# VectorE sums the softmax's exponents and takes their reciprocals behind all four low parts of the probabilities

## The reference, cut to what matters

```
q, k, v = xn @ Wq + bq, ctx @ Wk + bk, ctx @ Wv + bv     # xn is the normalised x; ctx is 8 x 1601 x 384
attn = softmax(q @ k.T / sqrt(32))                       # per batch and head: 64 x 1601
out  = attn @ v
x    = x + out @ Wo + bo
x    = x + moe(layernorm(x))                             # top 2 of 8 experts, 512 -> 2048 -> 512
```

## Time and profile before

| what | us |
|---|---|
| time, median of 3 runs | 1180.52 |
| the profiled execution's own time | 1178.61 |
| its span, first to last instruction | 1176.8 |
| TensorE busy | 1134.3 (96%) |
| VectorE busy | 980.9 (83%) |
| ScalarE busy | 728.4 (62%) |
| GpSimd busy | 499.8 (42%) |
| mean granted TensorE clock | 0.993 |

### The profile page before, as it was taken

How to read it: one execution, slowest core, us unless ns; L and a number is a source line. 1 busy time by engine, 2 the same in 40 slices (tenths; PEclk the granted TensorE clock), 3 DMA queues, 4 the chain that set the end, 5 groups by cost and what they waited for, 6 DMA issues and landing times.

```text
span 1176.8 us, 25102 instructions
## 1 busy us (share of the span) xinstructions
PE 1134.3 (96%) x8110; PEld 1081.3 (92%) x8110; DVE 980.9 (83%) x2286; ACT 728.4 (62%) x1505; POOL 499.8 (42%) x440
## 2 busy tenths in 40 slices
PE   4899999999999999999999999998999999999996
PEld 3799999999999999999999999986999999999996
DVE  6568888888889888888888888877888888888886
ACT  3455656656565656566565656654677777777774
POOL 6356555646546564655565564351112011111111
PEclk9899999999999999999999999999999999999999
DMA  5231212122121212121212211034787887878874
GB/s 185 82 92 42 64 54 60 57 59 60 43 72 40 64 49 64 47 65 46 62 40 72 64 40 44 27 130 144 215 270 234 267 247 235 234 244 270 239 234 117
DMA packets 82062, 137.49 MB, mean 117 GB/s; under 512 B 11513, under 2 KB 36217, under 8 KB 82033
## 3 DMA queue, kind: packets, MB, share of 16 engines
q1 hardware_dynamic: 78496, 129.12, 34.7%
q0 software_dynamic: 3536, 8.00, 3.4%
HBM read 129.96 MB, written 7.14 MB: 117 GB/s over the span
## 4 chain that ended last, share of the span: by engine, by line
PE 89%; DVE 5%; ACT 3%; issue 1%; DMA 1%; DVEq 1%; POOL 0%; ACTq 0%; SPq 0%; POOLq 0%
PE ps L1580 16%; PE ps L417 13%; PE ps L419 12%; PE ps L418 12%; PE ps L1426 8%; PE ps L1483 8%; PE ps L1581 6%; PE ps L1464 5%; PE ps L1465 4%; PE ps L1573 1%; PE ps L1415 1%; ACT y_gated L890 1%; PE ps L1616 1%; DMA wq_raw<-in_wq_dram 1%; DVE k_mix L987 1%
## 5 line engine op out<-in xcount | busy, mean ns | idle before, releaser
L555 POOL TENSOR_TENSOR ctx_hi<-ctx_raw,no_query 128x1152 fp32r<-128x1152 f32 x64 | 142.9, 2233 | 297.1 <-PE ps L419 287.5
L987 DVE SCALAR_TENSOR_TENSOR k_mix<-ps,bk_sb,k_mix 64x384 fp32r<-64x384 f32 (+1 forms) x256 | 162.2, 634 | 84.4 <-ACT k_mix L727 80.5
L767 ACT ACTIVATE probs<-ps,negmax 128x1152 f32<-128x1152 f32 x64 | 78.4, 1225 | 203.9 <-DVE negmax L1085 203.9
L417 PE MATMUL ps<-wv_hi,ctx_hi 128*128 128x256 f32 (+1 forms) x624 | 181.7, 291 | 6.7 <-DVE k_mix L987 6.5
L559 POOL TENSOR_TENSOR ctx_lo<-ctx_raw,ctx_hi 128x1152 fp32r<-128x1152 f32 x64 | 179.8, 2810 | 5.0
L419 PE MATMUL ps<-wv_hi,ctx_lo 128*128 128x256 f32 (+1 forms) x624 | 175.7, 282 | 0.0
L418 PE MATMUL ps<-wv_lo,ctx_hi 128*128 128x256 f32 (+1 forms) x624 | 175.2, 281 | 0.0
L727 ACT ACTIVATE k_mix<-ps,bk_sb 64x384 fp32r<-64x384 f32 (+1 forms) x256 | 150.9, 590 | 22.7 <-PE ps L419 18.0
L1580 PE MATMUL ps<-xg_mix,w_hi 128*128 128x320 f32 x584 | 163.3, 347 | 1.1 <-DVE h_sum L1262 1.1
L1580 PE MATMUL ps<-h_mix,w_hi 128*128 128x320 f32 x576 | 161.3, 349 | 2.7 <-DVE h_mix L1268 1.9
L1098 DVE TENSOR_TENSOR pt_mix<-ps,pt_mix 128x384 fp32r<-128x384 f32 (+1 forms) x256 | 138.7, 583 | 7.0 <-ACT pt_mix L778 5.0
(11 more groups left out here) (217 smaller groups left out, 2714.4 us busy)
## 6 DMA issues: line engine op xcount, KB each, us to landing
w_raw<-in_w_dram SPq DMA_DIRECT2D x76, 1024.0 KB, 6.1
ctx_raw<-in_ctx_t_dram SPq DMA_DIRECT2D x48, 576.0 KB, 3.8
ctx_raw<-in_ctx_t_dram SPq DMA_DIRECT2D x16, 673.5 KB, 4.1
out_dram<-acc POOLq DMA_DIRECT2D x2, 1024.0 KB, 10.6
q_both<-q_scratch SPq DMA_DIRECT2D x14, 128.0 KB, 3.0
x<-in_x_dram SPq DMA_DIRECT2D x1, 1024.0 KB, 5.6
wq_raw<-in_wq_dram SPq DMA_DIRECT2D x1, 1024.0 KB, 8.1
q_scratch<-q_out SPq DMA_DIRECT2D x1, 1024.0 KB, 6.2
```

The costliest lines, as they stand in the source:

```text
L417: pe.matmul(acc_ap, a_hi, b_hi, start=start, stop=False)
L555: nc.gpsimd.tensor_tensor(ctx_hi[slot][:, :, 0:n], ctx_raw[slot][:, :, 0:n], no_query[:].rearrange("p (o i) -> p o i", o=1).broadcast_to([ ...
L987: last = nc.vector.scalar_tensor_tensor(out=k_mix[other, 2 * a + i, cols], in0=ps[rows, bank, 0:m], scalar=bk_sb[rows, a:a + 1], in1=k_mix ...
```

## The change

The sum moves from in front of the four low parts to behind them, with its wait for the exponents, and the two reciprocals with their wait for the sum move from between the first and the second low part to behind the sum. Nothing else is changed, and the number of instructions is the same.

```diff
-                dve.wait_ge(exp_done, 2 * n + 2)
-                nc.vector.tensor_reduce(total[:], rowsum[:], AX.X, ALU.add).then_inc(total_ready, 1)
                 for c in range(CHUNKS):
                     dve.wait_ge(pt_high, CHUNKS * n + c + 1)
                     m = CHUNK_TILES[c]
                     nc.vector.tensor_tensor(pt_mix[:, TILE0[c]:TILE0[c] + m, 1, :],
                                             ps[:, SCORE_BANK + c, 0:m * P].rearrange("p (t r) -> p t r", t=m),
                                             pt_mix[:, TILE0[c]:TILE0[c] + m, 0, :].bitcast(F32),
                                             ALU.subtract).then_inc(pt_split, 1)
-                    if c == 0:
-                        dve.wait_ge(total_ready, n + 1)
-                        for h in range(2):
-                            rows = slice(h * HALF, (h + 1) * HALF)
-                            part = nc.vector.reciprocal(rinv_all[rows, h, s:s + 1], total[rows, :])
-                        part.then_inc(diag_ready, 1)
+                dve.wait_ge(exp_done, 2 * n + 2)
+                nc.vector.tensor_reduce(total[:], rowsum[:], AX.X, ALU.add).then_inc(total_ready, 1)
+                dve.wait_ge(total_ready, n + 1)
+                for h in range(2):
+                    rows = slice(h * HALF, (h + 1) * HALF)
+                    part = nc.vector.reciprocal(rinv_all[rows, h, s:s + 1], total[rows, :])
+                part.then_inc(diag_ready, 1)
                 if s == 0 and before is not None:
                     normalise(before[0])
```

## The result

The changed kernel takes 1183.32 us, median of 12 runs (1181.3 to 1184.0), against 1179.63 us for the kernel before, also 12 (1178.22 to 1181.28). The ratio is 1.0028, with a 95% interval of 1.0020 to 1.0035: 2.4 to 4.1 us slower. In the profiled executions the spans are 1180.0 and 1176.8 us, 3.2 apart. The forecast was 1181.2 us, +0.7, inside a range of -2.7 to +5.7. It had given that outcome, slower by more than 0.2%, 22%, and 68% to no change.

A forecast was written before the change was run, and what follows sets the result against it. VectorE and ScalarE were taken to pace ordinary steps, TensorE only steps 60 to 63. 7.1 - 5.9 - 0.2 - 0.3 = +0.7 us on 1180.5 gave 1181.2 us, range 1177.8 to 1186.2.

The forecast's parts named there:

- The ring: VectorE and ScalarE waiting on each other, negmax to negmax, 3.21 + 8.01 = 11.22 us, the whole ordinary step, without TensorE.
- The reading of the chain of waits, TensorE with 89%: Rival: TensorE is the bound, so low parts 0.41 earlier recover its stalls before the scores, -16.7 us, 1163.8 us; 3%.
- The longer tail: VectorE's stretch from early to late values grows from 2.76 to 2.88 us, 0.12 per step, 59 steps: +7.1 us.
- The bound above, L1036's 0.15: Upper bound for sum to reciprocal: the sum's 0.14 plus L1036's 0.15 to 0.16 start behind its awaited result, 0.30.
- The first steps of batches: First steps of batches 1 to 7 lose their waits for late TensorE, seven times 0.87: -6.1, without one branch -5.9 us.
- so all of it goes, and the late branch with it: In batches' first steps TensorE's lateness vanishes, 0.41 and 0.69 needed against 0.65 and 0.77 available, including the branch delay.
- the 0.08, 0.30 and 0.31: Waits for late TensorE in a batch's first step: before the keys' low parts, between key units, between the last two values.
- The branch's 0.18: Delay from last value to first maximum at the loop's branch, 0.51 against 0.33, claimed to come from the late value.
- Steps 59 to 63 and behind: Step 59 hides the added 0.12; steps 60 to 63 save 0.2 us; the fourth low part behind step 63 saves 0.34.
- The expert stage isn't touched: 0: The stage after attention was claimed to contribute no change, 0 us.
- TensorE's stops would grow: Sign to check: TensorE's stops before the scores at L1464 grow above 16.7 us instead of vanishing.
- The two rivals on the slower side: Dear wait between sum and reciprocal, 1187.7 us, 11%; batches' first steps don't recover, at most 1187.1 us, 11%.

The follow-up runs named there:

- `recips_behind`: The kernel before with only the two reciprocals and their wait moved behind the four low parts, the sum staying in front: 1175.57 us, ratio 0.9971.
- `twice`: The changed kernel with the sum made in two dependent stages, so its wait comes twice: 1191.71 us, ratio 1.0101 against the kernel before.
- `in_idle`: Against the kernel before, sum, wait and reciprocals moved in front of the keys' low parts, where VectorE waits anyway: 1168.22 us, ratio 0.9911.
- `only_six`: The change made only in step 6 of each batch, otherwise the kernel before: 1177.22 us, ratio 0.9978.
- `not_six`: The change made in all steps but step 6 of each batch: 1182.87 us, ratio 1.0035 against the kernel before.
- `covered`: The changed kernel with an extra, unused sum between the sum and its wait: 1182.18 us, ratio 1.0021 against the kernel before.
- the fillers: Seven unread matmuls in TensorE's 1.56 us idle time before gathering the first expert's rows: changed kernel 1181.63 us, kernel before 1179.97 us.

## Why the prediction was right in its mechanism and low in its size

**What bounds the kernel: right.** The ring paces ordinary steps. `recips_behind` moves the step by 0.00 us, and `twice` adds 0.18 to the changed kernel's, as the ring says to 0.01. `in_idle` takes 0.42 away as far as TensorE lets it, in the steps that come down to 10.80. The reading of the chain of waits, TensorE with 89%, is refuted by the changed kernel itself, by `recips_behind` (a gain of 3.4 us where it asked for some 10) and by `twice`. `in_idle` alone would fit it as well.

**The longer tail: right, a little low.** Forecast 0.12, measured 0.127 as the mean of the 52 steps among the 59 that aren't the first of a batch. For 59 that is 7.5 us and not 7.1. The terms are all as worked out (0.18 to the reciprocals, 0.36 from them to the late values): what was lost is within the rounding of rows with two decimals. The bound above, L1036's 0.15, played no part.

**The first steps of batches: the part that failed.** The step "so all of it goes, and the late branch with it" was half right. The 0.08, 0.30 and 0.31 that TensorE was late are gone, as the rows after show, and `only_six` and `not_six` show that step 6 is where most of it is decided, as argued. The branch's 0.18 stayed at 0.15. I took it for a result of the late value. That isn't enough: the second value starts on its own time and the maxima are still 0.15 late. The place of the branch is right, since the last first step, which lies behind the loop, has 0.33 there in both kernels. Why the 0.15 stay here and are gone in `twice`, no run shows. Seven first steps gave 7 x 0.71 = 5.0 us instead of 5.9.

**Steps 59 to 63 and behind: right in the sign, low in the size.** Step 59, forecast unchanged, became 0.1 shorter (12.21 to 12.11). For steps 60 to 63 and what lies behind, the forecast was -0.2 and -0.34. Measured are -0.3 for the last three distances (24.69 to 24.37), more than the 0.1 that the prediction named as the most to be seen, and -0.5 from the last `negmax` to the start of L1425 behind the last step. Counted from the first low part, as the forecast was, that start is 2.19 us behind instead of 2.54, so -0.35. It is now (answers to the earlier trace rows)

```profile
796.09 1.72 PE L1425 MATMUL ps<-pt_mix,v_mix 128*128 128x256 f32 x13 [0.55 <-issue]
```

**"The expert stage isn't touched: 0": wrong by 1.15 us.** No instruction there is touched, but the stretch of 1.2 GHz at the gathering was 3.4 us long before and 6.8 after. In sum, +0.7 became 7.5 - 5.0 - 0.1 - 0.3 - 0.5 + 1.15 = +2.75. With the 0.3 of loading and the 0.1 of the expert blocks it is the 3.2 of the spans.

**TensorE's stops would grow: wrong.** They fell from 16.7 to 8.7 us. TensorE's slack did grow, but elsewhere. By the distances between the starts of its matmuls, per batch, the scores take 12.9 us instead of 13.5, the projection of the values 28.9 instead of 28.2, and the transposes 11.0 instead of 10.9; the rest is equal. Against `in_idle`, where TensorE is the bound, it loses 1.8 us per batch in the changed kernel and lost 1.5 in the one before. Of this, the view of waits shows only the 12 waits at L417 for the keys' low parts, 1.9 us. As a test of the ring it was badly chosen.

**The two rivals on the slower side** didn't take place: the wait was not dear (0.035 behind the sum's end) and TensorE was not held up. The kernel came out at +0.28% by three terms of the forecast's own sum, each off in the same direction: 0.4 in the tails, 0.9 in the first steps, 1.15 by the clock; the small terms behind them took 0.4 off. Of the 3.3 us measured, 2.0 to 2.2 in the steps and -0.5 behind them can be called shown. The 1.15 by the clock came in 19 of 20 runs of the changed kernel, but it hangs on where the stretch falls and not on the steps: `covered`, with the same steps, has in 6 of its 10 runs the granted clock of the short stretch. With the fillers in both kernels the difference is 2.5 +- 1.5 us.

The sum's successor starts 0.07 behind it without a wait for it and 0.18 with one, and `covered` puts a whole instruction in between for nothing. The Trainium skill ("VectorE: DVE Perf Modes", section "The DRAIN you can't avoid") says that the next instruction starts only when the pipeline is empty and that a semaphore behind each costs nothing extra; the same section makes an exception for a next instruction that isn't held, which starts earlier. This pair falls under the exception, so here the wait costs 0.11 us, and where the prediction says that the trace disagrees with the rule it leaves the exception out.

The late values start 0.03 behind the end of the reciprocals, as the low part did before. The Trainium skill's rule in the section "Two Vector instructions with no wait between them" of the same page, on instructions that begin in another group of 32 partitions, agrees with that.

## What to carry to other kernels

Before moving a small instruction away from between others, look at what covers it. In this kernel a result that a neighbour waits for was nearly free with an independent instruction behind it (0.07 us) and cost its whole 0.18 us at the end of a group. Here moving two of the three (the reciprocals) gained 0.29%, moving all three lost 0.28%, and moving all three to a place where the engine waits anyway gained 0.89%. A ring of two engines can pace a kernel whose chain of waits shows a third with 89%; it shows by timelines whose period is the ring's length to the hundredth. And where a change of 0.3% is to be explained, compare the granted clock of the later stages first.

## What the runs showed of the hardware that was not expected

- TensorE, idle for 1.56 us behind small matmuls, ran the next matmuls partly at 1.2 GHz: for 3.4 us in six of ten profiles without fillers (both of the kernel before, `recips_behind`, `in_idle`, `not_six`, `covered`) and for 6.8 in four (both of the changed kernel, `only_six`, `twice`). With that idle time filled the granted clock stayed at 2.4 GHz in three of three. Where the stretch had begun 0.7 to 1.0 us ahead of the gathering it was 6.8 us long, where it began between 0.5 ahead and 0.75 behind, 3.4. So a shift of a microsecond in an earlier stage can move 1.1 to 1.6 us in a later one: `covered` has the changed kernel's steps and in its profile the short stretch, and from its last `negmax` to the end it takes 388.4 us against 389.9.
- A weight load's wait for a semaphore was only partly lost: 2.3 us of them per batch cost TensorE 1.5 us.
- The loop's branch cost VectorE 0.15 us between the second late value and the maxima (0.49 against 0.33) even when nothing there was late, and nothing in `twice`, where the step is 0.18 us longer (0.33 there). No run shows why.
